# Attention and FFN layer on one core: values' place in the step, a ring that runs on, and the order of the inverse sums' transfer

## The chip, the cores and the metric

The kernel runs on one core of one Trainium2 chip. The metric is the device time of one execution in microseconds, median of several runs; lower is better.

## What is computed

A transformer layer on x of 8 x 1024 x 256 in float32: layernorm, attention with 16 query heads and 4 key/value heads of width 16 (RoPE on q and k), output projection, layernorm and residual; then layernorm, a ternary-weight linear layer with bias, layernorm and residual. Cut to what matters here:

```
q = x @ Wq;  k = repeat(x @ Wk);  v = repeat(x @ Wv);  q, k = rope(q), rope(k)
scores = einsum('bhqd,bhkd->bhqk', q, k) / sqrt(256)
p = softmax(scores, axis=-1)
o = einsum('bhqk,bhkd->bhqd', p, v);  return o @ Wo
x = x + layernorm(attn(layernorm(x)))
x = x + layernorm(layernorm(x) @ ternary(weight).T * alpha + bias)
```

## The kernel before

The queries of each of the 8 batches are done in two halves of 512 (`qc` 0 and 1). A half has 32 steps, eight for each of the 4 head groups; a step takes one key tile of 128 for the four query heads of its group. All engines walk the same `Half` objects and are held together by semaphores; every engine executes its instructions in the order in which they are written, so a wait holds up all that stands behind it.

In a step, PE runs four pairs of matmuls. Each pair is one half of a maxima tile (`smax`, L995, keys against queries laid out by query row, for a head group 12 steps ahead, `LEAD`) and one score tile (`ring`, L1041) on other rows of the array, so that both run at once. DVE reduces each full 1024-wide smax tile to a row maximum (L1267), two a step; there are two smax buffers. The score tiles go through a ring of three PSUM slots (`RING`); ACT applies exp to each (L887) and writes `probs`, and that frees the slot. Row maxima come back into the score matmul as two extra rows of q: ACT and DVE split them into two fp16 parts, PE transposes them (job "MT", step 5 of eight), ACT copies them out to `max_rows`, and SP moves them into `q_rows` by two DMAs (L768). PE waits for these (`max_loaded`) at the first score of each head group.

The values (L1017, float32, four matmuls that share the array as four column tiles) multiply the `probs` of two steps before (`LAG`) into `pv`, either as a whole group of 512 columns or as two half groups of 256. `values_at` says where: before, a whole group behind pair four in a step that has a job behind pair two, and half groups behind pairs two and four in all others. At step 2, 10, 18 and 26 (`s % KT == LAG`) a new head group begins in `pv`, and its first group waits until ACT has read the old one (`read_heads`, L951).

Jobs stand behind pair two (`jobs_behind`), and each takes a ring slot which ACT empties: "XT" and "HT" are transposes of x and of the FFN's input, "Q", "K", "V" projections, "WO" the output projection (steps 8 to 11), "FF" the linear layer. The tables `PRO`, `PRO1` and `EPI` give them their steps. A half with qc = 0 has XT in steps 2 to 5, Q in 15 and 30 and K in 16; a half with qc = 1 has V in 5, 6, 7 and 16, Q in 15 and 30, and x statistics on DVE; both have WO, HT (20, 22) and FF (25, 27) of the half before. The second kind is called an A half below, the first a B half. The order is: the first half (qc = 0, with two XT each in steps 13 and 14), then A and B in turn up to the thirteenth, and three more (A, B without XT, and one without new projections).

`ring_free(n)` gives the number of evictions that must have been done before the n-th tile of a half may be written. The slot was `n % RING`, counted anew in each half; for the first three tiles of a half the wait was worked out from the counts of the halves before (`after`).

The sums of the exps come out of the values' matmul. Per pair of head groups, DVE inverts them (L1274, at `INVERT`: step 22 for pair 0, step 4 of the next half for pair 1), and SP writes them to DRAM (L724), waits until they have landed, and reads them back spread over the rows (L727, 256 KB). POOL multiplies (`scale_heads`, L577 `attnT`, at `SCALED`: step 27 and step 7). WO of step 8 waits for the second product of the half before (`divided`). SP is one queue: in step 5 and 21 it issues the maxima's rows, which wait for ACT's copy.

Of the kernel before, what the change touches and what calls it, by code (L numbers as in the profile page):

```python
# [101 lines left out]
INVERT, SCALED = {22: 0, 4: -1}, {27: 0, 7: -1}  # L102
# [37 lines left out]
class Half:  # L140


    def __init__(self, b, qc, scores=True, maxima=STEPS, turned=range(1, HKV + 1), pro=None, pro1=None,
                 epi=None, late=None, rot=None, base=0, first=0, steps=STEPS, load_x=None, mom=None, flush=True,
                 after=()):
# [20 lines left out]
        self.after = after  # L166
# [34 lines left out]
    def values_at(self, s):  # L201

        return {3: ALL} if self.jobs_behind(s, 1) else {1: (0, 1), 3: (1, 2)}
# [9 lines left out]
    def ring_free(self, n):  # L213

        if n >= RING:
            return self.base + n - RING + 1
        return self.base - min(((count - n - 1) % RING for count in self.after), default=0)
# [6 lines left out]
def sandwich_kernel(nc, x, wq, wk, wv, wo, wf, alpha, bias, rope_q, rope_k, out):  # L224
    ctx = ExitStack()
    with ctx:
# [139 lines left out]
        def schedule(half, eng, prepare=None):  # L366
# [14 lines left out]
            n0 = h.count  # L381
            n1 = Half(0, 1, pro1=0, epi=(0, 0)).count
            n2 = Half(0, 0, pro=0, epi=(0, 0)).count
            for b in range(B - 2):
                base = b * (n1 + n2) + at
                half(Half(b, 1, pro1=b + 1, epi=(b, 0), late=(b - 1, 1) if b > 0 else None, rot=(b + 1, 0),
                          base=base, mom=b + 2,
                          after=(n0, n2)))
                half(Half(b + 1, 0, pro=b + 2, epi=(b, 1), late=(b, 0), rot=(b + 1, 1), base=base + n1,
                          load_x=b + 3 if b + 3 < B else None, after=(n1,)))  # L390
            at += (B - 2) * (n1 + n2)
            h = Half(B - 2, 1, pro1=LAST, epi=(B - 2, 0), late=(B - 3, 1), rot=(LAST, 0), base=at, after=(n2,))
            half(h)
            at += h.count
            h = Half(LAST, 0, epi=(B - 2, 1), late=(B - 2, 0), rot=(LAST, 1), base=at, after=(h.count,))
            half(h)
            at += h.count
            h = Half(LAST, 1, epi=(LAST, 0), late=(B - 2, 1), maxima=STEPS - LEAD, turned=range(1, HKV), base=at,
                     after=(h.count,))
# [3 lines left out]
            h = Half(B, 0, scores=False, maxima=0, turned=(), epi=(LAST, 1), late=(LAST, 0), base=at,  # L403
                     after=(h.count,))
# [229 lines left out]
        def _(eng):  # L634
# [84 lines left out]

            def spread_inverses(h, pair):  # L720

                eng.wait_ge(inverted, h.pair0 + pair + 1)
                at_least(eng, divided, h.pair0 + pair)
                eng.dma_start(inv_dram[pair % DT, :, :].rearrange("j (k n) -> (j k) n", n=FOLD),  # L724
                              inv_sums[:, pair % DT, :]).then_inc(inv_stored, 16)
# [5 lines left out]
            def half(h):  # L731
# [9 lines left out]
                for s in h.steps:  # L741
# [13 lines left out]
                    if s in INVERT and (h.scores if INVERT[s] >= 0 else h.flush):  # L755
                        spread_inverses(h, INVERT[s])
# [6 lines left out]
                    if h.turns(s):  # L763
# [3 lines left out]
                        for side in range(2):  # L767
                            eng.dma_start(q_rows[side * SIDE + KROWS:side * SIDE + SROWS, qc, g * KVP:(g + 1) * KVP, :],  # L768
                                          max_rows[side * MROWS * KVP * ST:(side + 1) * MROWS * KVP * ST, nxt % 2, :])\
                               .then_inc(max_loaded, 16)  # L770
                    if h.scores and h.qc == 1 and s % KT == 0 and s > 0 and h.b is not LAST:

                        eng.wait_ge(ring_full, h.done("ST", s - 1, G - 1))
                        take_k(h.b + 1, s // KT - 1)
# [71 lines left out]
        def _(eng):  # L846
# [25 lines left out]
            def half(h):  # L872
                n = 0
                for s in h.steps:
# [7 lines left out]
                    for i, j in enumerate(JORDER):  # L882
                        if i == 2 and (s + LEAD) % KT == 0 and h.first < s <= h.maxima:
                            high_max(h, (s + LEAD) // KT - 1)
                        if h.scores:
                            eng.wait_ge(ring_full, h.done("ST", s, j))
                            eng.activation(probs[:, s % PSLOTS, j, :], ring[:, n % RING, :], ACT.Exp,  # L887
# [13 lines left out]
            def copy_jobs(h, jobs, n):  # L901
                for job in jobs:
                    kind, a = job[0], job[1:]
                    src = ring[:, n % RING, :]
# [51 lines left out]
        def _(eng):  # L956
# [66 lines left out]
            def half(h):  # L1023
                n = 0
                for s in h.steps:
# [5 lines left out]
                    for i, j in enumerate(JORDER):  # L1031
                        if s < h.maxima:
                            maxima(h, mg, mkt, 1 - i // 2, i % 2)
                        if h.scores:
# [6 lines left out]
                            eng.matmul(ring[:, n % RING, :],  # L1041
# [3 lines left out]
                            n += 1  # L1045
                        if i in parts:
                            values(h, s - LAG, *parts[i])
                        n = projections(h, h.jobs_behind(s, i), n)

            def projections(h, jobs, n):  # L1050
                for job in jobs:
                    kind, a = job[0], job[1:]
                    dst = ring[:, n % RING, :]
# [313 lines left out]
```

## Time and profile before

| | |
|---|---|
| median of 3 runs | 1492.5 us (1488.67 to 1494.1) |
| profiled execution, its own time | 1492.92 us |
| its span | 1491.1 us |
| PE busy | 1431.0 us (96%), 12350 matmuls |
| PE weight loads | 460.7 us (31%) |
| DVE busy | 1337.7 us (90%) |
| ACT busy | 1240.0 us (83%) |
| POOL busy | 754.6 us (51%) |
| mean granted TensorE clock | 0.978 |

The 16 halves fill the time from 77.6 to 1447 us; ahead of them lie loading, the first projections and the maxima of the first head groups, behind them the last half's output projection and FFN. The granted clock is full (2.4 GHz) in the halves. A timeline row gives start, duration, engine, line, operation, tiles and, in brackets, how long the engine was idle before it and what released it. PE and PEld are the matmul and the load of its weights.

### The profile page before, as it was taken

The page shows a single profiled execution, that of the slowest core. Times are in us where ns is not written, and L with a number is a line of the kernel's source. Part 1 is how long each engine was busy: PE and PEld are TensorE (multiplying, and loading weights), DVE is VectorE, ACT ScalarE, POOL GpSimd, SP SyncE. Part 2 cuts the span into 40 slices and gives each one's busy share as a digit, 9 for nine tenths or more (in the row PEclk, how much of TensorE's full clock was granted, in tenths as well). Part 3 has the DMA queues.
Part 4 walks back from the last instruction along what each step waited for, and adds up shares of the span by engine and source line. Part 5 has one row for each costly group of instructions (what it writes and reads, how often), then busy time and mean ns, then how long its engine had stood idle before and what let it go on. Part 6 is the DMA issues. An engine that isn't in the chain of part 4 may idle for free.

```text
span 1491.1 us, 32225 instructions
## 1 busy us (share of the span) xinstructions
PE 1431.0 (96%) x12350; PEld 460.7 (31%) x12350; DVE 1337.7 (90%) x1471; ACT 1240.0 (83%) x2483; POOL 754.6 (51%) x1205
## 2 busy tenths in 40 slices
PE   6699999999999999999999999999999999999996
PEld 5122322223232332323222233323322232222236
DVE  5798999999999999999999999999999989999814
ACT  2079889898988989898898989898898989899881
POOL 4322275645665466745656555745656455363340
PEclk9589999999999999999999999999999999999999
DMA  3311121311212130221313122221311112121001
GB/s 106 102 48 48 33 71 41 98 34 50 70 60 66 51 80 23 87 53 46 79 36 94 31 72 48 78 63 41 76 41 55 39 60 66 36 66 31 30 23 44
DMA packets 72921, 84.92 MB, mean 57 GB/s; under 512 B 17632, under 2 KB 58464, under 8 KB 71328
## 3 DMA queue, kind: packets, MB, share of 16 engines
q1 hardware_dynamic: 71952, 82.08, 19.7%
q8 instruction: 98, 1.61, 0.4%
q10 hardware_dynamic: 816, 0.79, 0.2%
q14 instruction: 55, 0.45, 0.1%
HBM read 46.66 MB, written 24.64 MB: 48 GB/s over the span
## 4 chain that ended last, share of the span: by engine, by line
PE 73%; ACT 12%; DVE 7%; issue 4%; POOL 2%; DMA 1%; SPq 0%; POOLq 0%; ACTq 0%; DVEq 0%
PE pv L1017 28%; PE smax L995 27%; ACT probs L887 10%; DVE row_max L1267 5%; PE ring L1130 5%; PE ring L1041 3%; PE ring L1104 3%; PE ring L1118 2%; PE ring L1138 2%; ACT heads L951 1%; PE ring L1124 1%; PE ring L1065 1%; PE ring L1088 1%; ACT act L940 1%; PE smax L961 0%
## 5 line engine op out<-in xcount | busy, mean ns | idle before, releaser
L1267 DVE TENSOR_REDUCE row_max<-smax 128x1 f32<-128x1024 f32 x1024 | 1202.0, 1216 | 82.6 <-PE smax L995 73.1
L887 ACT ACTIVATE probs<-ring 128x512 f32<-128x512 f32 x2048 | 1103.9, 598 | 114.2 <-PE ring L1041 91.7
L995 PE MATMUL smax<-k_rows,q_rows 48*128 48x512 f16 x2048 | 631.3, 389 | 14.4 <-DVE row_max L1267 5.9
L1041 PE MATMUL ring<-q_rows,k_rows 50*128 50x512 f16 x2048 | 637.6, 384 | 3.5 <-DMA q_rows<-max_rows 1.6
L1017 PE MATMUL pv<-probs,v_cols 128*32 128x256 f32 (+1 forms) x6520 | 610.8, 447 | 11.7 <-ACT heads L951 11.3
L995 PEld LDWEIGHTS smax<-k_rows,q_rows 48*128 48x128 f16 x2048 | 115.7, 94 | 493.4 <-issue 293.6
L1017 PEld LDWEIGHTS pv<-probs,v_cols 128*32 128x32 f32 x6520 | 128.7, 108 | 331.6 <-issue 180.9
L1041 PEld LDWEIGHTS ring<-q_rows,k_rows 50*128 50x128 f16 x2048 | 132.7, 93 | 54.8 <-ACT probs L887 46.3
L577 POOL TENSOR_TENSOR attnT<-pairs,inv_rows 128x512 f32<-128x512 f32 x31 | 39.5, 1273 | 178.6 <-DMA inv_rows<-inv_sums_dram 178.6
L556 POOL TENSOR_TENSOR act<-act,bias_sb 128x256 f32<-128x256 f32 x60 | 42.3, 728 | 115.4 <-ACT act L940 115.4
L1130 PE MATMUL ring<-wo_sb,attnT 128*128 128x256 f32 x256 | 72.2, 407 | 3.9 <-DVE attnT L577 1.7
L1130 PEld LDWEIGHTS ring<-wo_sb,attnT 128*128 128x128 f32 x256 | 44.0, 190 | 33.3 <-issue 23.9
L866 ACT ACTIVATE rot_in<-ring 128x512 f32<-128x512 f32 (+1 forms) x45 | 24.5, 550 | 33.1 <-PE ring L1104 15.6
L548 POOL CAST act_parts<-actT 128x512 f16<-128x512 f32 x30 | 18.3, 610 | 66.0 <-ACT actT L933 66.0
L866 ACT ACTIVATE act<-ring 128x256 f32<-128x256 f32 x64 | 24.5, 383 | 22.3 <-PE ring L1130 17.5
L951 ACT ACTIVATE heads<-pv 128x512 f32<-128x512 f32 x64 | 38.5, 601 | 4.3 <-PE pv L1017 4.3
L543 POOL TENSOR_TENSOR res<-res,act 128x256 f32<-128x256 f32 x60 | 41.6, 725 | 0.0
L1104 PE MATMUL ring<-x_parts,wq_parts 128*128 128x512 f16 x168 | 41.1, 381 | 0.0
L1260 DVE BATCH_NORM_STATS2 sf_bn<-act 128x6 f32<-128x256 f32 x64 | 25.2, 414 | 17.7 <-POOL act L556 17.7
L421 POOL TENSOR_TENSOR sy_mv<-sy_bn 128x4 f32<-128x4 f32 x15 | 3.1, 207 | 71.8 <-DVE sy_bn L1253 71.8
L961 PE MATMUL smax<-ident 128*128 128x128 f32 x232 | 29.6, 293 | 6.7 <-POOL v_cols L810 6.7
L567 POOL TENSOR_TENSOR res<-res,act 128x1024 f32<-128x1024 f32 x15 | 35.4, 2361 | 1.3
(166 smaller groups left out, 1130.0 us busy)
## 6 DMA issues: line engine op xcount, KB each, us to landing
q_stage_dram<-q_parts SPq DMA_DIRECT2D x45, 256.0 KB, 2.5
q_rows<-q_stage_dram SPq DMA_DIRECT2D x30, 384.0 KB, 5.9
x_in<-in_L_attn_x SPq DMA_DIRECT2D x8, 1024.0 KB, 6.1
pairs<-heads SPq DMA_DIRECT2D x64, 128.0 KB
inv_rows<-inv_sums_dram SPq DMA_DIRECT2D x32, 256.0 KB
res<-in_L_attn_x SPq DMA_DIRECT2D x16, 512.0 KB, 4.2
out<-res SPq DMA_DIRECT2D x15, 512.0 KB, 3.2
k_rows<-k_stage_dram SPq DMA_DIRECT2D x64, 96.0 KB, 3.2
```

The costliest lines, as they stand in the source:

```text
L543: eng.tensor_tensor(res[:, t, :], res[:, t, :], act[:, t, :], ALU.add).then_inc(y_added, 1)
L556: eng.tensor_tensor(act[:, t, :], act[:, t, :], bias_sb[:, :], ALU.add).then_inc(biased, 1)
L577: eng.tensor_tensor(attnT[:, pair % DT, :], pairs[:, pair % DT, :], inv_rows[:, pair % DT, :], ALU.mult)\
L866: eng.activation(dst, src, ACT.Copy, scale=unit).then_inc(ring_read, 1)
L887: eng.activation(probs[:, s % PSLOTS, j, :], ring[:, n % RING, :], ACT.Exp, scale=score_unit).then_inc(ring_read, 1)
L951: eng.activation(heads[:, g % 2, :], pv[:, :], ACT.Copy).then_inc(heads_read, 1)
L995: mm = eng.matmul(smax[:, side, c, :], q_rows[at:to, qc, kv * KVP + jp, qt * P:(qt + 1) * P], k_rows[at:to, kv, c * 512:(c + 1) * 512], st ...
L1017: mm = eng.matmul(pv[j * VCOLS:(j + 1) * VCOLS, cols], v_cols[:, g, kt, :], probs[:, s % PSLOTS, j, cols], start=(kt == 0 and first == 0), ...
L1041: eng.matmul(ring[:, n % RING, :], k_rows[at:to, g, kt * P:(kt + 1) * P], q_rows[at:to, h.qc, g * KVP + j // 2, :], start=True, stop=True)\
L1104: mm = eng.matmul(dst[:, :], wq_parts[:, wm, dt, a[1], :], x_parts[:, xm, dt, at:at + HALF], start=(k + dt == 0), stop=(k == len(PRODUCTS) ...
L1130: mm = eng.matmul(dst[:, 0:D], attnT[:, dt, a[0] * P:(a[0] + 1) * P], wo_sb[:, dt, :], start=(dt == 0), stop=(dt == DT - 1))
L1267: eng.tensor_reduce(row_max[:, g % 2, at:at + 1], smax[:, side, :, :].rearrange("p c n -> p (c n)"), AX.X, ALU.max).then_inc(max_read, 1)
```

## The change

Four things change. (1) `values_at`: a step with XT or HT has its values as two half groups again, the first behind the transposes, the second behind pair four; a step that begins a head group and has no job has them whole behind pair three, in front of pair four; steps with other jobs keep them whole behind pair four. For this the jobs behind pair two are now issued ahead of the values there. (2) The ring's slot is `(h.base + n) % RING`: it runs on over the halves, and the wait is the same for every tile; `after` goes. (3) SP's `spread_inverses` is cut in two: `store_inverses` at step 22 and 4 as before, and the read back at 23 and 5 (`SPREAD`), in step 5 behind the maxima's rows. (4) The wait for `divided` moves with the read back.

```diff
-INVERT, SCALED = {22: 0, 4: -1}, {27: 0, 7: -1}
+INVERT, SPREAD, SCALED = {22: 0, 4: -1}, {23: 0, 5: -1}, {27: 0, 7: -1}
...
     def values_at(self, s):
-        return {3: ALL} if self.jobs_behind(s, 1) else {1: (0, 1), 3: (1, 2)}
+        kinds = [job[0] for job in self.jobs_behind(s, 1)]
+        if kinds and "XT" not in kinds and "HT" not in kinds:
+            return {3: ALL}
+        if not kinds and s % KT == LAG:
+            return {2: ALL}
+        return {1: (0, 1), 3: (1, 2)}
...
     def ring_free(self, n):
-        if n >= RING:
-            return self.base + n - RING + 1
-        return self.base - min(((count - n - 1) % RING for count in self.after), default=0)
+        return self.base + n - RING + 1
...
-            def spread_inverses(h, pair):
+            def store_inverses(h, pair):
                 eng.wait_ge(inverted, h.pair0 + pair + 1)
-                at_least(eng, divided, h.pair0 + pair)
                 eng.dma_start(inv_dram[pair % DT, :, :].rearrange("j (k n) -> (j k) n", n=FOLD),
                               inv_sums[:, pair % DT, :]).then_inc(inv_stored, 16)
+
+            def spread_inverses(h, pair):
+                at_least(eng, divided, h.pair0 + pair)
                 eng.wait_ge(inv_stored, (h.pair0 + pair + 1) * 16)
                 eng.dma_start(inv_rows[:, pair % DT, :],
...
                     if s in INVERT and (h.scores if INVERT[s] >= 0 else h.flush):
-                        spread_inverses(h, INVERT[s])
+                        store_inverses(h, INVERT[s])
...
                     if h.turns(s):
...
+                    if s in SPREAD and (h.scores if SPREAD[s] >= 0 else h.flush):
+                        spread_inverses(h, SPREAD[s])
...
-                            eng.activation(probs[:, s % PSLOTS, j, :], ring[:, n % RING, :], ACT.Exp,
+                            eng.activation(probs[:, s % PSLOTS, j, :], ring[:, (h.base + n) % RING, :], ACT.Exp,
...
+                        if i == 1:
+                            n = projections(h, h.jobs_behind(s, i), n)
                         if i in parts:
                             values(h, s - LAG, *parts[i])
-                        n = projections(h, h.jobs_behind(s, i), n)
+                        if i != 1:
+                            n = projections(h, h.jobs_behind(s, i), n)
```

PE, a step with a transpose of x in a half with qc = 0 (L1065 is L1070 in the changed file, L1017 is L1019). Before, from the pair in front of the transposes:

```order
L995 MATMUL smax<-k_rows,q_rows 128x512
L1041 MATMUL ring<-q_rows,k_rows 128x512
L1065 MATMUL ring<-ident,x_in 128x128 x4
L995 MATMUL smax<-k_rows,q_rows 128x512
L1041 MATMUL ring<-q_rows,k_rows 128x512
L995 MATMUL smax<-k_rows,q_rows 128x512
L1041 MATMUL ring<-q_rows,k_rows 128x512
L1017 MATMUL pv<-probs,v_cols 32x512 x4
```

The same place now:

```order
L997 MATMUL smax<-k_rows,q_rows 128x512
L1043 MATMUL ring<-q_rows,k_rows 128x512
L1070 MATMUL ring<-ident,x_in 128x128 x4
L1019 MATMUL pv<-probs,v_cols 32x256 x4
L997 MATMUL smax<-k_rows,q_rows 128x512
L1043 MATMUL ring<-q_rows,k_rows 128x512
L997 MATMUL smax<-k_rows,q_rows 128x512
L1043 MATMUL ring<-q_rows,k_rows 128x512
L1019 MATMUL pv<-probs,v_cols 32x256 x4
```

Half of the values has moved from behind pair four to behind the transposes; a ninth row and a second group of values have come in.

PE, step 26, where a head group begins, between the whole values of step 25 and the first pair of step 27. Before:

```order
L995 MATMUL smax<-k_rows,q_rows 128x512
L1041 MATMUL ring<-q_rows,k_rows 128x512
L995 MATMUL smax<-k_rows,q_rows 128x512
L1041 MATMUL ring<-q_rows,k_rows 128x512
L1017 MATMUL pv<-probs,v_cols 32x256 x4
L995 MATMUL smax<-k_rows,q_rows 128x512
L1041 MATMUL ring<-q_rows,k_rows 128x512
L995 MATMUL smax<-k_rows,q_rows 128x512
L1041 MATMUL ring<-q_rows,k_rows 128x512
```

Now:

```order
L997 MATMUL smax<-k_rows,q_rows 128x512
L1043 MATMUL ring<-q_rows,k_rows 128x512
L997 MATMUL smax<-k_rows,q_rows 128x512
L1043 MATMUL ring<-q_rows,k_rows 128x512
L997 MATMUL smax<-k_rows,q_rows 128x512
L1043 MATMUL ring<-q_rows,k_rows 128x512
L1019 MATMUL pv<-probs,v_cols 32x512 x4
L997 MATMUL smax<-k_rows,q_rows 128x512
L1043 MATMUL ring<-q_rows,k_rows 128x512
```

Three pairs now stand in front of the first values of the group, and pair four behind all of them.

SP, steps 4 and 5 of a half with qc = 0, from the store of the inverse sums. Before:

```order
L724 DMA inv_sums_dram<-inv_sums 128x32 [waits divided,inverted]
L727 DMA inv_rows<-inv_sums_dram 128x1x512 [waits inv_stored]
L768 DMA q_rows<-max_rows 2x8x128 [waits ring_read]
L768 DMA q_rows<-max_rows 2x8x128
L699 DMA x_in<-in_L_attn_x 128x8x256 [waits ring_full]
```

Now:

```order
L720 DMA inv_sums_dram<-inv_sums 128x32 [waits inverted]
L768 DMA q_rows<-max_rows 2x8x128 [waits ring_read]
L768 DMA q_rows<-max_rows 2x8x128
L727 DMA inv_rows<-inv_sums_dram 128x1x512 [waits inv_stored,divided]
L696 DMA x_in<-in_L_attn_x 128x8x256 [waits ring_full]
```

The spread has moved behind the two transfers of the maxima's rows and behind their wait for ACT's copy.

## Rows read from the trace of the kernel before

**Rows 1.** Stage table, a B half and an A half (us: busy, instructions by engine)

```profile
591.20:677.90 86.70, 85.91 (x749) 25.39 (x746) 81.78 (x83) 78.05 (x156) 52.03 (x77) 1.00 0.23 66
...
677.90:763.40 85.50, 84.62 (x745) 26.72 (x746) 81.85 (x91) 76.34 (x154) 46.73 (x82) 1.00 0.20 53
```

**Rows 2.** Timeline of DVE in an A half (start us, us, engine, line, operation)

```profile
684.48 5.75 DVE L1267 TENSOR_REDUCE row_max<-smax 128x1 f32<-128x1024 f32 x5 [0.23 <-PE smax L995]
```

**Rows 3.** Timeline of PE, its loads and ACT, step 4 of a B half

```profile
602.03 0.39 PE L995 MATMUL smax<-k_rows,q_rows 48*128 48x512 f16 x1
...
602.53 1.08 ACT L887 ACTIVATE probs<-ring 128x512 f32<-128x512 f32 x2 [0.40 <-PE ring L1041]
...
602.57 0.65 PE L1065 MATMUL ring<-ident,x_in 128*128 128x128 f32 x4
...
603.16 0.39 PE L995 MATMUL smax<-k_rows,q_rows 48*128 48x512 f16 x1
...
603.67 0.09 PEld L1041 LDWEIGHTS ring<-q_rows,k_rows 50*128 50x128 f16 x1 [0.39 <-ACT probs L887]
...
603.99 1.07 PE L1017 MATMUL pv<-probs,v_cols 128*32 128x512 f32 x8
...
604.99 0.39 PE L995 MATMUL smax<-k_rows,q_rows 48*128 48x512 f16 x1
```

**Rows 4.** Timeline of PE, step 2 of an A half, a new head group

```profile
682.32 0.39 PE L995 MATMUL smax<-k_rows,q_rows 48*128 48x512 f16 x1
...
683.27 0.64 PE L1017 MATMUL pv<-probs,v_cols 128*32 128x256 f32 x8 [0.35 <-ACT heads L951]
...
683.84 0.39 PE L995 MATMUL smax<-k_rows,q_rows 48*128 48x512 f16 x1
...
684.95 0.39 PE L995 MATMUL smax<-k_rows,q_rows 48*128 48x512 f16 x1
```

**Rows 5.** Timeline of PE, end of step 5 of a B half

```profile
606.94 1.06 PE L1017 MATMUL pv<-probs,v_cols 128*32 128x512 f32 x8
...
607.82 0.22 PE L1059 MATMUL ring<-ident_h,max_parts 128*32 128x128 f16 x1
...
607.98 0.39 PE L995 MATMUL smax<-k_rows,q_rows 48*128 48x512 f16 x1
```

**Rows 6.** Timeline of PE, first step of a B half and of an A half

```profile
591.22 0.37 PE L1041 MATMUL ring<-q_rows,k_rows 50*128 50x512 f16 x1
...
591.62 0.39 PE L1041 MATMUL ring<-q_rows,k_rows 50*128 50x512 f16 x1
...
677.35 0.39 PE L995 MATMUL smax<-k_rows,q_rows 48*128 48x512 f16 x1
...
677.91 0.37 PE L1041 MATMUL ring<-q_rows,k_rows 50*128 50x512 f16 x1 [0.17 <-ACT probs L887]
```

**Rows 7.** Timeline, all engines, steps 4 to 8 of a B half, and of the last

```profile
607.78 0.65 SPq L727 DMA_DIRECT2D inv_rows<-inv_sums_dram  x1
...
608.48 1.37 SPq L768 DMA_DIRECT2D q_rows<-max_rows  x2
...
611.52 1.27 POOL L577 TENSOR_TENSOR attnT<-pairs,inv_rows 128x512 f32<-128x512 f32 x1 [2.55 <-DMA inv_rows<-inv_sums_dram]
...
612.94 1.13 PE L1130 MATMUL ring<-wo_sb,attnT 128*128 128x256 f32 x4
...
1130.93 1.10 PE L1130 MATMUL ring<-wo_sb,attnT 128*128 128x256 f32 x4 [0.63 <-POOL attnT L577]
```

**Rows 8.** Timeline, all engines, steps 5 to 8 of an A half

```profile
692.03 0.67 SPq L727 DMA_DIRECT2D inv_rows<-inv_sums_dram  x1
...
692.94 1.39 SPq L768 DMA_DIRECT2D q_rows<-max_rows  x2
...
695.74 1.27 POOL L577 TENSOR_TENSOR attnT<-pairs,inv_rows 128x512 f32<-128x512 f32 x1 [13.56 <-DMA inv_rows<-inv_sums_dram]
...
699.27 0.92 PE L1130 MATMUL ring<-wo_sb,attnT 128*128 128x256 f32 x3
```

More of the change, by code:

```diff
@@ L143, in __init__ @@
     def __init__(self, b, qc, scores=True, maxima=STEPS, turned=range(1, HKV + 1), pro=None, pro1=None,
-                 epi=None, late=None, rot=None, base=0, first=0, steps=STEPS, load_x=None, mom=None, flush=True,
-                 after=()):
+                 epi=None, late=None, rot=None, base=0, first=0, steps=STEPS, load_x=None, mom=None, flush=True):
         self.b, self.qc = b, qc
@@ L380, in schedule @@
             at += h.count
-            n0 = h.count
-            n1 = Half(0, 1, pro1=0, epi=(0, 0)).count
-            n2 = Half(0, 0, pro=0, epi=(0, 0)).count
             for b in range(B - 2):
[L385 to L392, printed above, removed]
+                h = Half(b, 1, pro1=b + 1, epi=(b, 0), late=(b - 1, 1) if b > 0 else None, rot=(b + 1, 0),
+                         base=at, mom=b + 2)
+                half(h)
+                at += h.count
+                h = Half(b + 1, 0, pro=b + 2, epi=(b, 1), late=(b, 0), rot=(b + 1, 1),
+                         base=at, load_x=b + 3 if b + 3 < B else None)
+                half(h)
+                at += h.count
+            h = Half(B - 2, 1, pro1=LAST, epi=(B - 2, 0), late=(B - 3, 1), rot=(LAST, 0), base=at)
             half(h)
             at += h.count
-            h = Half(LAST, 0, epi=(B - 2, 1), late=(B - 2, 0), rot=(LAST, 1), base=at, after=(h.count,))
+            h = Half(LAST, 0, epi=(B - 2, 1), late=(B - 2, 0), rot=(LAST, 1), base=at)
             half(h)
             at += h.count
-            h = Half(LAST, 1, epi=(LAST, 0), late=(B - 2, 1), maxima=STEPS - LEAD, turned=range(1, HKV), base=at,
-                     after=(h.count,))
+            h = Half(LAST, 1, epi=(LAST, 0), late=(B - 2, 1), maxima=STEPS - LEAD, turned=range(1, HKV), base=at)
             half(h)
             at += h.count
-            h = Half(B, 0, scores=False, maxima=0, turned=(), epi=(LAST, 1), late=(LAST, 0), base=at,
-                     after=(h.count,))
+            h = Half(B, 0, scores=False, maxima=0, turned=(), epi=(LAST, 1), late=(LAST, 0), base=at)
             half(h)
@@ L903, in copy_jobs @@
                     kind, a = job[0], job[1:]
-                    src = ring[:, n % RING, :]
+                    src = ring[:, (h.base + n) % RING, :]
                     eng.wait_ge(ring_full, h.done(*job))
@@ L1040, in half @@
                             at, to = j % 2 * SIDE, j % 2 * SIDE + SROWS
-                            eng.matmul(ring[:, n % RING, :],
+                            eng.matmul(ring[:, (h.base + n) % RING, :],
                                        k_rows[at:to, g, kt * P:(kt + 1) * P],
@@ L1052, in projections @@
                     kind, a = job[0], job[1:]
-                    dst = ring[:, n % RING, :]
+                    dst = ring[:, (h.base + n) % RING, :]
                     at_least(eng, ring_read, h.ring_free(n))
```

1 line of the change is left out of this document (removed).

## Prediction

> **What bounds the kernel now.** I read the stage table first, then the timeline of single steps. A half is 32 steps; "A halves" are those of qc = 1 (value projections in steps 5 to 7), "B halves" those of qc = 0 that transpose x in steps 2 to 5. Seven A halves, six B halves, the first half and the last two make up the 16. In a B half DVE is busy for 81.78 of 86.70 us, in an A half for 81.85 of 85.50 [rows 1]: at most 4.9 and 3.7 us of a half can be won before DVE is the bound, whatever PE does. A plain step is twice the same half step: two smax/ring pairs, 0.54 us up to what follows [rows 3], and half a group of values, 0.57 up to the next pair [rows 4], 1.11 together. DVE, which must read one 1024-wide tile per half step, needs 5.75 / 5 = 1.15 in a row [rows 2], a little less where the ends overlap. So DVE slips some 0.03 behind PE per half step, and PE meets a wait when the slip has used up the second smax buffer, after about 0.3 us; later WO, V, Q or FF steps, longer for PE than for DVE, give it back. A gain of PE is worth something only where DVE is not behind at that place.
>
> **Values in halves beside transposes.** The step from 602.03 takes 2.96 us [rows 3]. Its PE work without waits: two pairs up to the transposes 0.54, the transposes 0.59 (602.57 to 603.16, the next pair), two pairs 0.54, a whole group 1.00: 2.67. The other 0.29 is the fourth pair's wait for a ring slot, which ACT had not emptied (0.39 of load idle, [rows 3]). The change puts half of the values in front of pair three, so the slot is free in time: ACT ends the ring tile of pair two at 603.61, 1.58 into the step, and pair four now comes at 1.9. In exchange there is one more group. A half group takes 0.57 from its start to the next pair [rows 4], two make 1.14 against 1.00. What transposes directly followed by values take has no row. Bounds: both pay their own overhead, 0.59 + 0.57 = 1.16, or the overhead of one is hidden, 0.59 + 0.44 = 1.03. The step is then 0.54 + 1.16 + 0.54 + 0.57 = 2.81, or 2.68. I take 2.81, a gain of 0.15, because of the nearest contrary case: the small transpose of the maxima (128*32, as wide as the values) behind a whole group makes 606.94 to 607.98 = 1.04 out of 1.00 (603.99 to 604.99) [rows 3, 5], nearly free, but it keeps the width of 32 columns, while x's transposes are 128 wide. The Trainium skill ("TensorEngine Tiling (Array Packing)", Key Properties) says that changing the tiling mode, not just the tile, drains TensorE, which speaks against this part of the change: one more change of mode per step. By that rule the step is 2.81, without it 2.68, 24 x 0.13 = 3 us over the B halves; rows 5 agree as far as they go. Per B half: step 2, where the whole values and ACT's read of the heads fall together, gains about 0.4, steps 3 to 5 0.15 each, and 0.1 goes again in steps 6 and 7, because DVE's second tile of an XT step is full 0.4 later and it starts the plain steps behind. 0.75 x 6 = **4.5**; the two double steps of the first half, 0.3. The 30 steps with the FFN's transposes (20 and 22) have the same form, but step 20 follows a new head group that leaves DVE late (below), and step 22 has no ring wait left to remove. Between 0 and 0.15 each; I take 0.05: **1.5**.
>
> **Whole in front of pair four at a new head group** (steps 2, 18, 26 without jobs, 9 + 15 + 15, and four in the first half). Now: step start 682.32, values at 683.27 after waiting 0.35 for the heads (0.95 instead of 0.54), next step 684.95, 2.63 in all [rows 4]. With the change pair three fills the wait: values still at 0.95, pair four at 1.95, next step at 2.18. PE would gain 0.45. But the second smax tile now closes with pair four, at 1.95 + 0.38 = 2.33; now DVE, idle for 0.23, starts on it at 684.48, 2.16 into the step [rows 2]. DVE starts it at 2.37, ends near 3.59; pair three of the next step, due at 2.18 + 1.11 = 3.29, needs that buffer and waits to about 3.65; the step after begins near 3.65 + 1.11 = 4.76 against 2.63 + 2.22 = 4.85. So 0.1 is left to PE, and DVE is 0.21 later. Bounds per place: gain 0.45, loss 0.21. I take **0**, since the steps behind are plain ones or have statistics on DVE.
>
> **Ring runs on.** At the start of an A half the smax matmul goes at 677.35, the ring matmul only at 677.91, 0.56 later, waiting for the slot [rows 6]; that comes of counting the ring anew, and DVE is idle there. 7 x 0.55 = 3.9. At the start of a B half (and of the last half but one) pair two comes 0.40 behind pair one (591.62 against 591.22) where half of the 0.54 would do, up to 0.2 late, and pair one waits a little itself [rows 6]: 7 x 0.25 = 1.7. Together **5.6**, PE's own and not eaten by DVE before step 2. Lower bound 0 if an ACT wait takes its place, but exps start 0.48 apart (1.08 for two that overlap, [rows 3]) and are ahead.
>
> **Inverse sums behind the maxima's rows.** This is the part that costs. In a B half SP issues the spread at 607.78, waits for ACT's copy of the maxima's transpose, and issues its two transfers at 608.48 for 1.37 us; POOL starts attnT at 611.52, 3.74 after the spread's issue, and ends at 612.79; WO of step 8 begins at 612.94, at once behind [rows 7]. There is no slack. The new order is rows first: spread at 608.48 + 1.37 + 0.04 = 609.89, POOL at 613.63, attnT done at 614.90, WO at 615.03. PE is in order, so everything behind WO waits: 2.1 us, and step 8 is then followed by PE-bound steps, so none comes back. One of the six, the last (1130.93), already waits 0.63 for attnT [rows 7] and loses about 1.3. 5 x 2.1 + 1.3 = **11.8**. In an A half the V steps give more room: spread at 692.94 + 1.42 = 694.36, POOL 3.71 later at 698.07, done 699.34, WO at 699.48 against 699.27 [rows 8]; 0.2 here, and by the scatter of a DMA's way up to half a microsecond elsewhere, 0.3 x 7 = 2.1. The last half but one about 0.6: **14.5** in all. What is gained, maxima's rows landing earlier, hides under the same WO wait. At steps 22/23 the B half's spread goes behind four K swap transfers, some 3 us of issue; attnT is then due only for the next WO, POOL has idle time there: 0.
>
> **Sum.** 4.5 + 0.3 + 1.5 + 0 + 5.6 = 11.9 won, 14.5 lost: +2.6 on the profiled execution (span 1491.1, own time 1492.92), which lies 0.4 over the median of the three runs, 1492.5. Forecast against that median: **1495.1 us**. Its own range, with the bounds on the transposes (3 less), the FFN steps (1.5 more to 3 less) and the stall of step 8 (1.5 either way): 1488 to 1498. About 0.5%, 7.5 us, is what a measurement of this kernel can tell from no change.
>
> **Rivals.**
> - *The heads' wait comes back whole.* DVE's slip would be harmless and the head-group steps keep their 0.45 (0.2 at step 26): 24 x 0.4 + 15 x 0.2 = 12.6 less, 1482.5. For: DVE is idle for 3.7 to 4.9 us per half. Against: the hand-walk above, with the buffer coming free at 3.59. Chance 0.07.
> - *attnT is not late*, because POOL does not need the 3.7 us or the rows are issued earlier than I read. Then 14.5 is not lost: 1480.6. For: with 2 us of PE wait in sight a small shift of issue matters. Against: SP's rows stand 1.37 apart in all halves, and the WO start of 612.94 leaves no room. Chance 0.12.
> - *DVE pays for the later second tile* at each of the 43 head-group steps: 0.21 x 43 = 9.0 more, 1504.1. The point that decides: whether DVE has at least 0.21 of idle time between a head group and the next one. For: 94 and 96% busy in the two kinds of half, and rows 2 show five tiles in a row right behind the group. Against: PE-bound WO, V and FF steps follow each. Chance 0.13.
> - *No extra drain* (2.68): 1492.0, inside the forecast's side, chance 0.23; *forecast* 0.45.
> The spread and the ring do what they say; I see no way in which the edit is void.
>
> **Numbers.** Faster by over 0.5% needs one of the first two rivals: 0.19. Slower by over 0.5% needs 1500.0 and more: the DVE rival, 0.13. Same: 0.68. The range reaches from the edge of the fast cases to half of the slow one, 1484 to 1501.
>
> **What would show it.** Right: step 8 of the B halves 5.2 us instead of 3.13, with PE waiting on POOL's attnT, some 14 us in total; XT steps 2.8; no gap between smax and ring at a half's start; head-group step 2.2 and the one behind it 2.6; POOL's attnT starting 3.7 us behind the spread. Wrong: WO in B halves without a wait, or DVE's total idle time larger by more than the WO waits.

## The result, and the profile after

The changed kernel takes **1514.8 us** (median of 4 runs, 1513.0 to 1515.8), the kernel before beside it 1491.1 us: a ratio of 1.0156, 95% interval 1.0133 to 1.0180. That is 1.6% slower. The forecast was 1495.1, with a range of 1484 to 1501: 2.6 us over the kernel before, where 23.7 were measured. The profiled execution has an own time of 1515.83 us and a span of 1514.0, against 1492.92 and 1491.1.

The page of the changed kernel: span, busy times, the chain by engine, and two groups with their idle time.

```profile
span 1514.0 us, 32433 instructions
...
PE 1428.3 (94%) x12454; PEld 463.5 (31%) x12454; DVE 1326.0 (88%) x1471; ACT 1240.9 (82%) x2483; POOL 756.6 (50%) x1205
...
PE 59%; DVE 19%; issue 12%; POOL 5%; ACT 3%; DMA 1%; SPq 0%; POOLq 0%; DVEq 0%; ACTq 0%
...
L1272 DVE TENSOR_REDUCE row_max<-smax 128x1 f32<-128x1024 f32 x1024 | 1201.3, 1216 | 118.7 <-PE smax L997 115.7
...
L1135 PE MATMUL ring<-wo_sb,attnT 128*128 128x256 f32 x256 | 76.1, 424 | 20.3 <-POOL attnT L574 19.6
```

Before, WO (the last row; line 1130 there) was 72.2 us busy and idle for only 3.9 us ahead of it. Now it waits 19.6 us for POOL's attnT, and takes 3.9 us more for the same 256 matmuls. A wait does not make a matmul longer: that second number is the trail of the main miss. A second change stands in the waits of the maxima's matmul for the row maximum, before and after (23.0 us for 5.9):

```profile
L995 PE MATMUL smax<-k_rows,q_rows 48*128 48x512 f16 x2048 | 631.3, 389 | 14.4 <-DVE row_max L1267 5.9
L997 PE MATMUL smax<-k_rows,q_rows 48*128 48x512 f16 x2048 | 629.8, 390 | 33.9 <-DVE row_max L1272 23.0
```

The stage table for the B half and the A half of [rows 1] (columns as there):

```profile
597.16:687.61 90.45, 87.28 (x780) 26.27 (x778) 80.03 (x83) 77.86 (x156) 51.82 (x77) 0.96 0.23 63
687.61:773.81 86.20, 84.33 (x742) 26.64 (x740) 81.81 (x91) 76.63 (x155) 47.23 (x83) 1.00 0.20 53
```

The B half has grown from 86.70 to 90.45 us, the A half from 85.50 to 86.20, and in the B half the granted clock is no longer 1.00 but 0.96.

**Where it goes in a B half.** The timeline of all engines answers to [rows 7]:

```profile
613.43 1.35 SPq L768 DMA_DIRECT2D q_rows<-max_rows  x2
...
614.88 0.66 SPq L727 DMA_DIRECT2D inv_rows<-inv_sums_dram  x1
...
618.95 1.26 POOL L574 TENSOR_TENSOR attnT<-pairs,inv_rows 128x512 f32<-128x512 f32 x1 [4.92 <-DMA inv_rows<-inv_sums_dram]
...
620.36 2.05 PE L1135 MATMUL ring<-wo_sb,attnT 128*128 128x256 f32 x4 [2.23 <-POOL attnT L574]
...
622.34 0.60 PE L997 MATMUL smax<-k_rows,q_rows 48*128 48x512 f16 x1
...
623.31 1.93 PE L1019 MATMUL pv<-probs,v_cols 128*32 128x512 f32 x8
```

The order and the wait are as forecast: first the maxima's rows, then the spread; attnT starts 4.07 us behind the spread's issue, and WO comes 2.23 us late. But then four WO matmuls take 2.05 us where they took 1.13 [rows 7], a smax matmul 0.60 for 0.39, a group of values 1.93 for 1.07 [rows 3]. The windows of the same stretch (the number ahead of the last two is PEclk):

```profile
605.00:617.50 12.50, 12.50 (x131) 4.04 (x129) 11.59 (x13) 11.92 (x25) 6.19 (x7) 1.00 0.18 59
617.50:620.30 2.80, 0.63 (x8) 0.11 (x4) 1.96 (x2) 1.52 (x3) 1.35 (x2) 0.88 1.00 332
620.30:627.10 6.80, 6.74 (x24) 2.46 (x24) 2.08 (x2) 2.56 (x5) 6.72 (x6) 0.55 0.09 28
627.10:632.00 4.90, 4.90 (x34) 1.42 (x32) 4.37 (x6) 4.39 (x9) 3.75 (x3) 1.00 0.09 28
```

TensorE is full up to 617.5 and stands for 2.2 of the next 2.8 us. Towards the end of this wait, at 619.6, the granted clock falls from 2.4 to 1.2 GHz and stays there for 6.8 us (0.55 is mostly the lower level), of which TensorE works through all but the first 0.8. Step 8, measured from its first smax matmul to that of step 9, is 7.65 us here; in the six B halves it is 6.98, 5.29, 7.65, 7.18, 6.77 and 6.85, where the forecast had 5.2. The second one is the control: nearly the same wait, and no fall of the clock (its timeline, and its window from WO's start). In the six halves WO waits 2.22, 2.12, 2.23, 2.49, 2.73 and 2.10 us, and the stretches at 0.5 last 3.4, none, 6.8, 3.4, 3.4 and 3.4 us.

```profile
441.26 0.65 SPq L727 DMA_DIRECT2D inv_rows<-inv_sums_dram  x1
...
445.21 1.26 POOL L574 TENSOR_TENSOR attnT<-pairs,inv_rows 128x512 f32<-128x512 f32 x1 [4.80 <-DMA inv_rows<-inv_sums_dram]
...
446.62 1.10 PE L1135 MATMUL ring<-wo_sb,attnT 128*128 128x256 f32 x4 [2.12 <-POOL attnT L574]
```

```profile
446.60:453.00 6.40, 6.38 (x41) 2.28 (x42) 4.05 (x5) 4.45 (x10) 6.32 (x6) 1.00 0.13 43
```

In an A half the wait is short, as forecast, and nothing follows it (timeline, answers to [rows 8]):

```profile
704.50 0.66 SPq L727 DMA_DIRECT2D inv_rows<-inv_sums_dram  x1
...
708.32 1.27 POOL L574 TENSOR_TENSOR attnT<-pairs,inv_rows 128x512 f32<-128x512 f32 x1 [15.79 <-DMA inv_rows<-inv_sums_dram]
...
709.74 1.10 PE L1135 MATMUL ring<-wo_sb,attnT 128*128 128x256 f32 x4 [0.34 <-POOL attnT L574]
```

**The head-group step**, which answers to [rows 2, 4] (timeline of PE, its loads and DVE, step 2 of an A half):

```profile
691.70 2.35 DVE L1272 TENSOR_REDUCE row_max<-smax 128x1 f32<-128x1024 f32 x2
692.04 0.39 PE L997 MATMUL smax<-k_rows,q_rows 48*128 48x512 f16 x1
...
692.97 0.39 PE L997 MATMUL smax<-k_rows,q_rows 48*128 48x512 f16 x1 [0.33 <-DVE row_max L1272]
...
693.29 1.06 PE L1019 MATMUL pv<-probs,v_cols 128*32 128x512 f32 x8
...
694.52 0.38 PE L997 MATMUL smax<-k_rows,q_rows 48*128 48x512 f16 x1
...
694.72 5.75 DVE L1272 TENSOR_REDUCE row_max<-smax 128x1 f32<-128x1024 f32 x5 [0.67 <-PE smax L997]
...
696.00 0.39 PE L997 MATMUL smax<-k_rows,q_rows 48*128 48x512 f16 x1 [0.31 <-DVE row_max L1272]
...
697.22 0.37 PE L997 MATMUL smax<-k_rows,q_rows 48*128 48x512 f16 x1
```

Pair three was to come at 0.54 in front of the heads' wait. It comes at 0.93 (692.97), because the smax tile that it writes is still being read by DVE: two reads of 1.18 us each began at 691.70. With pair three the tile behind it comes late too: DVE starts on it at 694.72, 2.68 into the step, after 0.67 of idleness, where it was 2.16 and 0.23 [rows 2], and pair three of the next step waits for DVE again (0.31). The values begin at 1.25 instead of 0.95, the step is 2.48 and the next one 2.70: 5.18 us for the two, where they were 2.63 + 2.21 = 4.84 and were forecast at 4.76 to 4.85.

**The transposing step**, which answers to [rows 3] (timeline of PE, step 4 of a B half):

```profile
604.41 0.39 PE L997 MATMUL smax<-k_rows,q_rows 48*128 48x512 f16 x1
...
604.99 0.66 PE L1070 MATMUL ring<-ident,x_in 128*128 128x128 f32 x4
605.57 0.64 PE L1019 MATMUL pv<-probs,v_cols 128*32 128x256 f32 x8
...
606.14 0.39 PE L997 MATMUL smax<-k_rows,q_rows 48*128 48x512 f16 x1
...
606.68 0.64 PE L1019 MATMUL pv<-probs,v_cols 128*32 128x256 f32 x8
...
607.25 0.39 PE L997 MATMUL smax<-k_rows,q_rows 48*128 48x512 f16 x1
```

0.58 + 1.15 + 0.54 + 0.57 = 2.84 us; it was 2.96, and the forecast built 2.81 from the same four pieces.

**All steps together.** Differences of the step lengths, after minus before, summed over the kernel's halves (us; 32 steps x 16 halves, each step here counted from its first score matmul to the next step's):

| part | forecast | measured |
|---|---|---|
| XT, steps 2 to 7 of the B halves, and steps 13 and 14 of the first half | -4.8 | -4.1, all in the B halves |
| HT, steps 20 to 25 | -1.5 | -1.2 |
| whole values at 43 head-group places (and the step behind) | 0 | +7.8 |
| ring, half starts | -5.6 | -4.8 |
| spread: B halves | +11.8 | +22.1 |
| spread: A halves | +2.1 | +2.4 |
| spread: last two halves, step 8 | +0.6 | +4.0 |
| steps 4 to 7 of the last two halves | 0 | -1.9 |

They sum to +24.3; 1.4 us of that go again ahead of the first and behind the last half, and the span is 22.9 longer. The last two halves' rows belong together: in the kernel before their step 7 was longer, by 0.6 and 1.6 us, so taken together steps 4 to 8 are 2.3 us longer in the last half but one and 0.2 shorter in the last.

### The profile page after: what moved, and what is told of

It is laid out like the page before. It is cut to its first block, busy times and chain, and to the rows that moved or that the text cites. A ratio compares the mean times of both kernels' runs of the same rounds, so it can differ in the third digit from the quotient of the medians.

```text
span 1514.0 us, 32433 instructions
## 1 busy us (share of the span) xinstructions
PE 1428.3 (94%) x12454; PEld 463.5 (31%) x12454; DVE 1326.0 (88%) x1471; ACT 1240.9 (82%) x2483; POOL 756.6 (50%) x1205
## 4 chain that ended last, share of the span: by engine, by line
PE 59%; DVE 19%; issue 12%; POOL 5%; ACT 3%; DMA 1%; SPq 0%; POOLq 0%; DVEq 0%; ACTq 0%
PE pv L1019 23%; PE smax L997 22%; DVE row_max L1272 16%; PE ring L1135 5%; ACT probs L889 3%; PE ring L1109 2%; PE ring L1143 2%; PE ring L1043 1%; POOL attnT L574 1%; PE ring L1129 1%; PE ring L1093 1%; PE ring L1070 1%; POOL res L564 1%; POOL act L436 1%; DVE sy_bn L1258 1%
## 5 line engine op out<-in xcount | busy, mean ns | idle before, releaser
L1043 PE MATMUL ring<-q_rows,k_rows 50*128 50x512 f16 x2048 | 628.7, 385 | 0.2
L1019 PE MATMUL pv<-probs,v_cols 128*32 128x256 f32 (+1 forms) x6624 | 616.7, 444 | 0.5 <-ACT probs L889 0.4
L997 PEld LDWEIGHTS smax<-k_rows,q_rows 48*128 48x128 f16 x2048 | 119.4, 94 | 533.6 <-DVE row_max L1272 269.6
L1019 PEld LDWEIGHTS pv<-probs,v_cols 128*32 128x32 f32 x6624 | 131.0, 108 | 315.8 <-issue 182.9
L1135 PE MATMUL ring<-wo_sb,attnT 128*128 128x256 f32 x256 | 76.1, 424 | 20.3 <-POOL attnT L574 19.6
L1143 PE MATMUL ring<-wfT,act_parts 128*128 128x256 f16 x256 | 33.3, 274 | 3.7 <-ACT probs L889 3.7
```

The costliest lines, as they stand in the source:

```text
L997: mm = eng.matmul(smax[:, side, c, :], q_rows[at:to, qc, kv * KVP + jp, qt * P:(qt + 1) * P], k_rows[at:to, kv, c * 512:(c + 1) * 512], st ...
L1019: mm = eng.matmul(pv[j * VCOLS:(j + 1) * VCOLS, cols], v_cols[:, g, kt, :], probs[:, s % PSLOTS, j, cols], start=(kt == 0 and first == 0), ...
L1043: eng.matmul(ring[:, (h.base + n) % RING, :], k_rows[at:to, g, kt * P:(kt + 1) * P], q_rows[at:to, h.qc, g * KVP + j // 2, :], start=True, ...
L1135: mm = eng.matmul(dst[:, 0:D], attnT[:, dt, a[0] * P:(a[0] + 1) * P], wo_sb[:, dt, :], start=(dt == 0), stop=(dt == DT - 1))
L1143: mm = eng.matmul(dst[:, t * D:(t + 1) * D], act_parts[:, m, dt, at:at + P], wfT[:, dt, :], start=(k == 0), stop=(k == 2 * DT - 1))
```

## Experiments

Theory at the start: the time lies in two places, the late spread (half of it wait, half of it the clock that falls behind the wait) and the whole values at a head group; ring and halves do what the forecast says. Rival: the edits only hurt in company, or the clock falls for a reason of its own. Each run stands beside runs of the kernel before on the same chip.

**1. The changed kernel with the spread back behind its store.**

```diff
                         store_inverses(h, INVERT[s])
+                        spread_inverses(h, INVERT[s])
...
-                    if s in SPREAD and (h.scores if SPREAD[s] >= 0 else h.flush):
-                        spread_inverses(h, SPREAD[s])
```

> The changed kernel with one part undone: the spread of the inverse sums is issued right behind their store again (steps 22 and 4), ahead of the maxima's rows. Theory (attnT late for WO in step 8, and TensorE's clock granted at half behind the long wait): step 8 of the B halves goes back from about 7 us to 3.1, no stretch at half clock inside the halves, 26 us less than the change: about 1489. Rival (the late spread costs only its 2.1 us of wait per B half, and the rest is lost elsewhere): 14 less, about 1500.

Measured: 1486.7 us (12 runs), ratio 0.9979 (0.9969 to 0.9990), granted clock 0.981 against 0.971. The theory holds: this edit costs 1514.8 - 1486.7 = 28.1 us (26 by the two ratios, since the two times come from different chips), and the others together gain 3 us. Step 8 of the B halves is 3.2 to 4.4 us, and from 87 to 1479 us no stretch of the trace is below full clock.

**2. The changed kernel without whole values at a new head group.**

```diff
-        if not kinds and s % KT == LAG:
-            return {2: ALL}
```

> The changed kernel with one part undone: the first values of a head group are two half groups again. Theory (a whole group in front of pair four holds DVE's second tile and pair three back): 7 us less than the change, about 1508; steps 2 and 3 of an A half 2.6 and 2.2 instead of 2.48 and 2.70. Rival (it costs nothing, the rows of steps 3 and 19 only show a shift): within 2 us of the change.

Measured: 1508.9 us (4 runs), ratio 1.0130 (1.0106 to 1.0154). 5.9 us come back, and steps 2 and 3 of an A half are 2.63 and 2.21 again. The clock falls in all six B halves here.

**3. Both back: only the ring and the halves beside transposes are left.**

> The changed kernel with both undone, so that the running ring and the halves beside the transposes alone stay. Theory: the kernel before minus 4.8 for the ring and 4 to 5 for the transposes, minus 1: about 1481 to 1482 against 1491. Rival (these gains are eaten by DVE as soon as the others are gone): 1488 or more.

Measured: **1477.9 us** (6 runs), ratio 0.9923 (0.9907 to 0.9940), 3 to 4 us better than expected; no stretch at 0.5 lies between 86 and 1468 us, not even the one that the kernel before has in its last half (run 7). WO waits for POOL 1.6 us in the whole kernel:

```profile
L1132 PE MATMUL ring<-wo_sb,attnT 128*128 128x256 f32 x256 | 71.3, 403 | 3.5 <-POOL attnT L572 1.6 <-ACT probs L886 1.0 <-DVE attnT L572 0.8
```

**4. The kernel before with the spread alone moved.** The diff is the reverse of 1, on the kernel before.

> The kernel before with only the inverse sums' spread moved behind the maxima's rows. Theory: the loss does not depend on the other parts: 22 to 26 more than before, 1513 to 1517, with step 8 of the B halves near 7 us and half-clock stretches behind it. Rival (it needs the shorter steps of the change to be late): under 12 more.

Measured: 1517.6 us (5 runs), ratio 1.0182 (1.0162 to 1.0202): 27.7 us, the same price as in 1, so it needs no company. Step 8 of the B halves is 7.95, 8.82, 5.20, 7.31, 5.63 and 6.09 us; the halves with 5.20 and 5.63 show no stretch at 0.5 behind the wait. WO waits 2.54, 3.41, 2.03, 2.84, 2.46 and 1.88 us in them: the clock stays up behind 2.46 and falls behind 1.88, so the length of the wait does not decide it by itself. The row of the waits for attnT (us in all, times, the longest):

```profile
PE ring L1135 <- POOL attnT L577: 21.1, 14, 3.4
```

**5. The wait filled with work, too much of it.** The clock was so far a reading of rows. Here the wait stays as it is and TensorE does something in it, in all halves with qc = 0 that have a WO: the six B halves and the last but one.

```diff
+                        if a[0] == 0 and h.qc == 0 and h.scores:
+                            for _ in range(FILL):
+                                eng.matmul(dst[:, 0:P], ident[:, :], ident[:, :], start=True, stop=True)
```

> The changed kernel with 18 extra matmuls of the identity (128x128 into 128 columns) issued on TensorE into the output projection's ring slot between its wait for the slot and its wait for the divided values, in the halves of query chunk 0 with scores. Nothing is left out: the extra products are overwritten by the projection. Theory (the 2.2 us in which TensorE stands still before the output projection takes its granted clock to half for 3.4 or 6.8 us): the wait itself stays, since the divided values come when they come, but it holds work, so that no stretch at 0.5 follows in these halves; step 8 of them is then 5.2 to 5.6 us, as in the one half in which the clock did not fall, instead of 6.8 to 7.7, so 6 x 1.6 = about 10 us less: 1503 to 1507 us. Rival (the long step is only the wait and what is queued behind it, the clock falls for another reason): no less than the changed kernel, 1512 to 1518, and stretches at 0.5 still there.

Measured with FILL = 18: 1517.0 us (4 runs), ratio 1.0180 (1.0154 to 1.0206). By its time this is the rival's result. The timeline of a B half shows why:

```profile
618.30 4.29 PE L1135 MATMUL ring<-ident 128*128 128x128 f32 x36
...
622.42 1.03 PE L1138 MATMUL ring<-wo_sb,attnT 128*128 128x256 f32 x4
```

18 products of f32 are 36 matmuls and take 4.29 us, twice the wait. They replaced the wait of 2.2 us and the slow stretch behind it by 4.1 us of their own, from 618.30 to WO's start. No stretch at 0.5 is left in these halves (granted clock 0.981), WO takes 1.03 us, and step 8 is 7.15 in every one of them. The run was mis-sized and says only half of what it should; so once more, to size.

**6. The same with FILL = 9.**

> The changed kernel with 9 extra matmuls of the identity instead of 18 in the same place (in the run with 18 they took 4.29 us, from 618.30 to 622.59, so that they themselves held the output projection up by 2 us beyond its wait: 9 take 2.1 us, about the wait's own length). Nothing is left out: the products are overwritten. Theory (the wait takes the granted clock to half, and that is the rest of the long step): no stretch at 0.5 in these halves, step 8 of them 5.2 to 5.8 us instead of 6.8 to 7.7, 6 x 1.6 = about 10 us less than the changed kernel: 1503 to 1508 us. Rival (only the wait and its queue): 1512 to 1518.

Measured: **1504.6 us** (4 runs), ratio 1.0091 (1.0076 to 1.0105), within the theory's 1503 to 1508 and 10.2 us under the changed kernel. The same place, timeline and windows:

```profile
614.74 2.28 PE L1135 MATMUL ring<-ident 128*128 128x128 f32 x18
615.89 1.26 POOL L574 TENSOR_TENSOR attnT<-pairs,inv_rows 128x512 f32<-128x512 f32 x1 [5.17 <-DMA inv_rows<-inv_sums_dram]
...
617.21 1.13 PE L1138 MATMUL ring<-wo_sb,attnT 128*128 128x256 f32 x4 [0.19 <-POOL attnT L574]
...
618.80 1.07 PE L1019 MATMUL pv<-probs,v_cols 128*32 128x512 f32 x8
```

```profile
614.00:616.80 2.80, 2.80 (x30) 2.17 (x22) 2.14 (x2) 1.70 (x4) 0.91 (x1) 1.00 1.01 309
616.80:624.00 7.20, 7.01 (x44) 2.66 (x44) 4.43 (x5) 4.84 (x10) 7.12 (x7) 1.00 0.13 42
```

attnT comes just as late, WO starts just as late, and everything behind it runs at 1.00. Step 8 is 5.52, 5.14, 5.59, 5.58, 5.46 and 5.14 us. The kernel does more work and is 10 us faster. So of the spread's 28 us some 10 are the clock in the seven halves that were filled. The other 18 are the waits and a stretch at 0.5 that is left in the last half, which was not filled: 3.4 us from 1396.7 on, behind a wait of 2.02 us.

**7. The kernel before with whole values at a new head group alone.**

> The kernel before with one edit: at the first step of a head group without a projection between the scores and the values, all the values stand in front of pair four. Theory (the second score buffer is read later than forecast, so that pair three waits longer than the moved values save): steps 2 and 18 with those behind them gain 0.2 to 0.35 us of length each, step 26 loses 0.1, about 7 us over the kernel: 1495 to 1498 us. Rival 1 (the forecast: nothing at all): 1490 to 1492. Rival 2 (the loss appears only together with the other edits): 1489 to 1492 also, and step 2 and 18 no longer than before.

Measured: 1492.3 us (10 runs), ratio 1.0010 (0.9998 to 1.0023). By the time, the forecast's zero (rival 1), and the theory's 1495 to 1498 is missed. By the steps it is the theory: steps 2 and 3 of an A half are 2.41 + 2.70 = 5.11 here for 4.84, and the head-group places together are 7 us longer. What gives it back stands elsewhere: steps 6 to 8 of the last two halves are 4.7 us shorter. In the kernel before the last half has a wait and a slow stretch of its own. The section on the profile before says that the clock is full in the halves; in this one it is not (timeline of PE, then windows, of the kernel before):

```profile
1383.66 0.39 PE L1041 MATMUL ring<-q_rows,k_rows 50*128 50x512 f16 x1 [1.32 <-DMA q_rows<-max_rows]
...
1384.85 1.50 PE L1130 MATMUL ring<-wo_sb,attnT 128*128 128x256 f32 x3 [0.59 <-ACT probs L887]
```

```profile
1382.50:1385.00 2.50, 0.75 (x4) 0.29 (x5) 1.37 (x2) 0.85 (x2) 1.26 (x1) 1.00 0.06 22
...
1385.00:1388.40 3.40, 3.40 (x12) 1.21 (x16) 0.96 (x2) 1.65 (x4) 0.00 (x0) 0.50 0.00 0
```

TensorE stands for 1.75 of 2.5 us, waiting for the maxima's rows among other things, and then runs at 0.50 for 3.4 us. Here the steps ahead of it are longer, the wait for the rows has shrunk, and the stretch is gone. That the one follows from the other is a reading of the trace; no run tried it. Nor do all executions of the kernel before seem to have that stretch: of the 17 beside this run, six have a mean granted clock of 0.980 or 0.981 and take 1487.2 to 1492.2 us, the others 0.976 to 0.979 and 1489.4 to 1494.9, while the ten of this kernel all have 0.980 or 0.981. The profiled one, with 0.978, is of the slower kind, so that a difference from its last half is not a difference in the medians.

**8. The kernel before with halves beside transposes alone.**

```diff
-        return {3: ALL} if self.jobs_behind(s, 1) else {1: (0, 1), 3: (1, 2)}
+        kinds = [job[0] for job in self.jobs_behind(s, 1)]
+        if kinds and "XT" not in kinds and "HT" not in kinds:
+            return {3: ALL}
+        return {1: (0, 1), 3: (1, 2)}
...
+                        if i == 1:
+                            n = projections(h, h.jobs_behind(s, i), n)
                         if i in parts:
                             values(h, s - LAG, *parts[i])
-                        n = projections(h, h.jobs_behind(s, i), n)
+                        if i != 1:
+                            n = projections(h, h.jobs_behind(s, i), n)
```

> The kernel before with one edit: beside key and query transposes (jobs XT and HT) the values are in halves, in front of pairs two and four, and the projection's jobs come ahead of the values. Theory: XT steps 2.80 to 2.85 us instead of 2.95, step 2 of those halves 2.82 instead of 3.25, of which steps 6 and 7 give back 1 us or so of 5: 4 to 5 us off with the transposes of heads' 1 us: 1485 to 1487 us. With the ring edit the sum was 1477.9, so the ring edit is then worth the rest, 7 to 9 us. Rival (the two edits help each other: without the ring edit's freed start the halves gain nothing): 1489 to 1491.

Measured: 1481.7 us (6 runs), ratio 0.9937 (0.9918 to 0.9956), 3 us better than expected. That the ring would then be worth 7 to 9 us was wrong too: it is 5 (run 9). Steps 2 to 5 of the B halves give 5.0 us and lose 2.4 again in steps 6 to 8; the HT steps give 1.1. Another 3.5 us come from the last half: its steps 7 and 8, from score to score, are 2.28 and 3.48 us where they were 3.92 and 5.35, and no stretch at 0.5 is there (windows of this kernel, steps 7 and 8 of the last half):

```profile
1374.00:1380.50 6.50, 6.18 (x56) 1.84 (x52) 6.03 (x6) 5.72 (x12) 1.28 (x1) 1.00 0.12 43
```

Why the rows are in time here, although no step grew, is not settled. Some executions of the kernel before may not have lost this time either (run 7).

**9. The kernel before with the ring alone.**

> The kernel before with the ring edit alone (the ring's slots run on from half to half, each half starts where the last one stopped). Theory: the first scores of a half of query chunk 0 no longer wait for a slot freed late, 6 x 0.65 + 0.9 over the others = 4.8 us off, as measured with the other edits: 1485 to 1487 us. Rival (with the ring edit alone the time comes back at step 8 of the halves of query chunk 0, since the divided values are then waited for earlier): 1488 to 1491. The forecast's own size was 5.6.

Measured: 1485.7 us (6 runs), ratio 0.9961 (0.9946 to 0.9975): 5.0 us less, as the theory had it. The slow stretch of the last half is still in this trace.

**10. The kernel of run 3 with whole values at the last head group of a half alone.**

```diff
+        if not kinds and s == 3 * KT + LAG:
+            return {2: ALL}
```

> Ring edit and halves beside transposes as in the kernel with both others undone (1477.9 us), and the values whole in front of pair four at the start of the last head group of a half (step 26) alone. Theory (what it does depends on when the second score buffer is read: at step 26 steps 26 and 27 together were 0.09 to 0.11 us shorter in the changed kernel, at the others 0.22 to 0.34 longer): 15 x 0.1 = 1.5 us less, 1475.5 to 1477.5. Rival (whole values cost at each group start): 1479 to 1481.

Measured: **1475.3 us** (6 runs), ratio 0.9896 (0.9877 to 0.9916), the best of all. In its trace steps 26 and 27 are 2.01 + 3.40 = 5.41 us for 2.46 + 3.05 = 5.51 in run 3, 1.4 us over the kernel. Here the step ahead, 25 with the FFN's matmuls, is long (3.05 us), so that DVE has caught up: it stands idle for 0.31 us in step 26, and pair three finds its tile free, 0.44 into the step. The difference from run 3's time, 2.6 us, is between two chips and not much above the scatter; the sign at step 26 stands in the trace.

## Why the prediction was wrong, by its own steps

- **"Inverse sums behind the maxima's rows", 5 x 2.1 + 1.3 = 11.8 in the B halves: mechanism right, price short by 10.** The order of SP's issues, the way to attnT (3.7 us forecast, 3.9 to 4.6 in the six halves) and the wait (2.1 us forecast, 2.1 to 2.7 measured) are all there, and run 6, in which only the wait is left, has 12.6 us in step 8 of these halves. The term that failed is the silent one: that behind the wait TensorE goes on at the speed it had. It goes on at half, for 3.4 or 6.8 us, in five halves of six. "So none comes back" was true, and more goes.
- **"The last half but one about 0.6": +2.7 in step 8, 2.3 over steps 4 to 8.** Same cause: WO waits 1.81 us and a stretch at 0.5 lies there, at 1323. The last half, which the forecast left out, has the same at 1408 (a wait of 1.91 us), but in the kernel before it had a slow stretch too, at 1385, so its steps 4 to 8 come out 0.2 shorter. On the page that stretch is no more than a rounding of the clock row, and the forecast took the clock in the halves as full. The windows of the kernel before show, ahead of any change, what less than 2 us of standing still can do here.
- **"Whole in front of pair four": "I take 0", measured +7.8 over the 43 places** (5.9 between the changed kernel and run 2, 8.9 between runs 1 and 3). The walk put pair three at 0.54 "in the wait"; it asked when DVE would read the second tile and not when DVE would be done with the one that pair three writes. [rows 4] don't show that; the DVE row ahead of that of [rows 2] does (timeline of DVE, kernel before), two reads of 1.18 us of which the first ends at 683.09, 0.77 into the step:

```profile
681.91 2.35 DVE L1267 TENSOR_REDUCE row_max<-smax 128x1 f32<-128x1024 f32 x2
```

  The rival "DVE pays for the later second tile" had the right engine, the right sign and 9.0 us, and got 0.13. Its tile does come later, by 0.52 in an A half where it counted 0.21, because pair three is held up as well; that its total came so near is in part luck.
- **Right:** XT with 2.81 (2.80 to 2.85 measured), -4.1 for -4.5 in the B halves, though nothing for -0.3 in the first half; HT -1.2 for -1.5; the A halves' wait, +2.4 for +2.1 (one WO waits 0.34 us). The drain that the Trainium skill ("TensorEngine Tiling (Array Packing)", Key Properties) gives for a change of mode agrees with the trace: transposes and half a group of values take 1.15 us together, not the 1.03 of hidden overhead. No run separates the change of mode from other overhead.
- **Ring: -5.6 forecast, -4.8 in the trace, -5.0 in run 9.** One of the A halves, the one behind the last B half, had no gap at its start before, so it is six times 0.55 and not seven; the B halves' starts give 0.25 each as put.
- **The rivals** all moved one known term. None had a wait that changes the speed of what follows, and so the range ended at half of the DVE rival. The clock by itself is worth 10 us and the head groups 8: on top of the forecast's 1495.1 either one alone ends 2 to 4 us above the range and both together 12, at 1513; 1514.8 was measured.

## What to carry to other kernels

Where an edit makes TensorE stand for about 2 us in a stretch that was full, price the wait twice: its length, and the work behind it at the lower clock, which this kernel's rows show for 3.4 or 6.8 us; ask for the granted clock by windows around every wait that is already there before the edit. When a write is pulled forward past a wait, check who still reads the buffer that it writes, not only who will read it next. And undo the parts one by one even if the whole is slower: the ring and the halves beside transposes were worth 12 us together, 1477.9 against 1489.9, and whole values at the last head group alone perhaps some more.

## What the runs showed of the hardware

- One wait of 2.1 to 2.7 us, with TensorE full ahead of it (12.5 of 12.5 us in the place shown) and behind it, went with a fall of the granted clock from 2.4 to 1.2 GHz in five of six B halves of the changed kernel, for 3.4 or 6.8 us, in all six of run 2 and in four of six of run 4. Waits of 2.12 us (changed kernel), 2.03 and 2.46 (run 4) left it alone and one of 1.88 (run 4) did not, so a single place does not tell; what decides it stays open. In run 1, where WO waits 0.63 us at most, it never falls in the halves. The Trainium skill ("TensorE: Matmul & The Clock Gate", HAM oscillation — how this bites in real kernels) describes waits for a DMA after which the next work starts cold. The trace agrees in that: behind a single wait per half, here for POOL, WO and what follows run at 1.2 GHz.
- Matmuls whose result nobody uses, 9 products of f32 in 2.28 us in that wait (18 matmuls in the trace), kept the clock at 1.00 and made the kernel 10.2 us faster.
- At 1.2 GHz the rows are longer, but do not double: WO's four matmuls 2.05 for 1.13 us, values 1.93 for 1.07, a smax matmul 0.60 for 0.39. The ends in such rows are modelled; from start to start, from WO to the first pair behind the values, it is 4.81 us at 1.2 GHz and 2.57 at 2.4 (the half at 446).
- The way from the spread's issue to POOL's start scatters by some tenths of a microsecond: 3.6 to 4.2 us in the B halves of the kernel before, 3.9 to 4.6 in those of the changed one, where the spread stands behind the rows. It moves every wait of this kind with it.
